# A four-layer retention kernel: both chunks' keys by values in one VectorE operation, a ring of four states, both states formed one behind the other

## What is computed

```python
Q = _rotate(Q, cos, sin); K = _rotate(K, cos, -sin)
att = jnp.einsum('bnhd,bmhd->bhnm', Q, K) * Dm      # Dm[n, m] = gamma**(n-m) for n >= m, else 0
Y = jnp.einsum('bhnm,bmhd->bnhd', att, V)
Y = (Y - mean) * rsqrt(var + EPS) ...
return G * Y @ Wo
```

## Time and profile before

| | us |
|---|---|
| median of 3 runs | 592.39 |
| the three runs | 592.39, 590.1, 597.42 |
| the profiled execution | 590.93 |
| its span, first to last instruction | 589.1 |
| mean granted TensorE clock, as a share of full speed | 0.979 |

### The profile page before, as it was taken

The page is one execution under the profiler, slowest core; times in us unless marked ns, Lnnn a source line. Parts: engine busy times, 40 slices in busy tenths (PEclk is TensorE's granted clock), DMA queues, the critical chain, the costliest instruction groups (busy, mean ns, idle before and its releaser), DMA issues. The chain is left out here.

```text
span 589.1 us, 13981 instructions
## 1 busy us (share of the span) xinstructions
PE 523.4 (89%) x4372; PEld 409.7 (70%) x4372; DVE 495.6 (84%) x1824; ACT 362.3 (61%) x830; POOL 214.1 (36%) x223
## 2 busy tenths in 40 slices
PE   0788999999999999999968896996499999897994
PEld 0656787878888888888856564994255777456992
DVE  6799999999999999999978897788958999993653
ACT  2577888787888887887747594686144310132760
POOL 2343543543543543543530073474200000072661
PEclk9899999999999999999999999899699999998998
DMA  8979999993000000000000311323000000012315
GB/s 305 364 201 187 182 171 183 181 177 59 3 1 2 2 3 2 2 2 2 2 1 2 116 47 54 87 65 104 0 0 1 2 0 2 0 52 59 101 56 160
DMA packets 61129, 43.29 MB, mean 73 GB/s; under 512 B 4640, under 2 KB 58272, under 8 KB 60800
## 3 DMA queue, kind: packets, MB, share of 16 engines
q1 hardware_dynamic: 56160, 35.42, 30.7%
q0 software_dynamic: 2496, 5.13, 2.6%
q10 hardware_dynamic: 2400, 1.84, 1.0%
HBM read 18.38 MB, written 24.01 MB: 72 GB/s over the span
## 5 line engine op out<-in xcount | busy, mean ns | idle before, releaser
L544 POOL TENSOR_TENSOR qk<-cosq,sinq 128x512 f32<-128x512 f32 x32 | 44.0, 1376 | 164.2 <-DVE cosq L865 164.2
L524 POOL TENSOR_TENSOR att<-att,small 128x512 f32<-128x512 f32 x63 | 79.0, 1275 | 10.2 <-ACT att L360 10.1
L368 ACT ACTIVATE xz<-resid,nmr,rs 128x128 f32<-128x128 f32 x128 | 53.1, 482 | 15.5 <-DVE nmr L921 15.4
L1234 POOL DMA_INDIRECT rows_back<-ffn_yt,ffn_front x46 | 47.8, 1038 | 40.5 <-DVE ffn_yt L1585 36.5
L1414 PE MATMUL banks<-ffn_xtT,ffn_wt 128*128 128x128 f32 x368 | 51.6, 286 | 2.0 <-DVE ffn_hr L1579 2.0
L1414 PEld LDWEIGHTS banks<-ffn_xtT,ffn_wt 128*128 128x128 f32 x368 | 47.1, 200 | 2.8 <-ACT ffn_wt L1261 2.2
L809 DVE TENSOR_TENSOR att<-banks,small 128x512 f32<-128x512 f32 x64 | 43.9, 685 | 4.9 <-PE banks L583 3.9
L1086 PE MATMUL banks<-small 128*128 128x512 f32 (+1 forms) x74 | 31.7, 547 | 13.6 <-POOL osc_taps L1657 11.5
L1225 POOL DMA_INDIRECT rows_in<-ffn_front,ffn_slot x32 | 31.9, 998 | 29.0 <-DVE ffn_slot L1497 20.5
L1217 POOL MEMSET ffn_all_one<- 128x8 f32 x2 | 0.2, 104 | 107.6 <-POOLq L1649 83.8
L360 ACT ACTIVATE att<-banks 128x512 f32<-128x512 f32 x63 | 37.9, 603 | 0.5 <-PE banks L583 0.5
(11 more groups left out here) (259 smaller groups left out, 1430.5 us busy)
## 6 DMA issues: line engine op xcount, KB each, us to landing
rows_in<-zero_rows SPq DMA_DIRECT2D x16, 1032.0 KB, 19.2
shared_tab<-in_rot SPq DMA_DIRECT2D x3, 1024.0 KB, 12.5
routed_sb<-in_routed SPq DMA_DIRECT2D x1, 3072.0 KB, 12.4
ffn_front<-rows_in SPq DMA_DIRECT2D x46, 64.5 KB, 1.8
ffn_yg<-rows_back SPq DMA_DIRECT2D x8, 256.0 KB, 3.7
shared_tab<-in_rot ACTq DMA_DIRECT2D x1, 1024.0 KB, 10.0
w<-in_W SPq DMA_DIRECT2D x2, 512.0 KB, 7.4
times<-in_times SPq DMA_DIRECT2D x1, 1024.0 KB, 4.9
```

Source lines behind the costliest of these rows:

```text
L368: ins = act.activation(xz[:, n], resid[:, (g % GROUPS) * 2 + n % 2], ACT.Identity, scale=rs[:, n:n + 1], bias=nmr[:, n:n + 1])
L524: pool.tensor_tensor(att[:, c, HALF:HEADS], att[:, c, HALF:HEADS], spread(causal.unsqueeze(1), 1, HALF), ALU.mult) \
L544: pool.tensor_tensor(qk[:, v].rearrange("p a b c -> p (a b c)"), cosq[:].rearrange("p a b -> p (a b)"), sinq[:].rearrange("p a b -> p (a b ...
L1234: pool.indirect_dma_start(rows_back, bass.IndirectOffsetOnAxis(ap=token, axis=0), yt[:, j % RING], None).then_inc(stored[j % RING], 16)
```

## The change

`keys_values` takes both chunks in one VectorE operation on 128 x 256 elements, with the mask repeated over the two chunks. Where a group is the last of its layer (first + 2 = 16, four groups of 32) the two chunks have different decays, and two operations stay, one behind the other. `kv_taken` counts groups and no longer chunks. The states go round in four buffers, and both `new_state` of a group stand one behind the other in the step in which its first stood before.

```diff
-        state = sb("state", [P, 2, D])
+        STATES = 4
+        state = sb("state", [P, STATES, D])
...
-                        pe.matmul(b_y[:, c * P:c * P + P], state[:, c], qkT[:, v, 0, c], start=(c == 0), stop=False,
+                        pe.matmul(b_y[:, c * P:c * P + P], state[:, (2 * g + c) % STATES], qkT[:, v, 0, c], start=(c == 0), stop=False,
...
-                            wait(pe, s["kv_taken"], 2 * (t - 1))
+                            wait(pe, s["kv_taken"], t - 1)
...
-                def keys_values(g, c):
-                    wait(dve, s["state_ready"], 2 * g + c - 1)
+                def keys_values(g):
+                    wait(dve, s["state_ready"], 2 * g)
                     wait(dve, s["kv_ready"], g + 1)
-                    dve.scalar_tensor_tensor(out=kvm[:, c], in0=b_og[:, c * P:c * P + P],
-                                             scalar=chunk_decay(g, c), in1=block,
-                                             op0=ALU.mult, op1=ALU.mult).then_inc(s["kv_taken"], 1)
+                    both = b_og[:, 0:2 * P].rearrange("p (c n) -> p c n", c=2)
+                    first = (2 * g) % NCH
+                    if first + 2 < NCH:
+                        dve.scalar_tensor_tensor(out=kvm[:], in0=both, scalar=decay[:, first:first + 1],
+                                                 in1=spread(block.unsqueeze(1), 1, 2),
+                                                 op0=ALU.mult, op1=ALU.mult).then_inc(s["kv_taken"], 1)
+                    else:
+                        for c in range(2):
+                            ins = dve.scalar_tensor_tensor(out=kvm[:, c], in0=both[:, c],
+                                                           scalar=decay[:, first + c:first + c + 1], in1=block,
+                                                           op0=ALU.mult, op1=ALU.mult)
+                        ins.then_inc(s["kv_taken"], 1)
 
                 def new_state(g, c):
-                    wait(dve, s["kv_taken"], 2 * g + c + 1)
+                    wait(dve, s["kv_taken"], g + 1)
                     wait(dve, s["state_ready"], 2 * g + c)
-                    wait(dve, s["state_read"], 2 * g + c)
-                    dve.scalar_tensor_tensor(out=state[:, 1 - c], in0=state[:, c],
-                                             scalar=chunk_decay(g, c), in1=kvm[:, c],
+                    wait(dve, s["state_read"], 2 * g + c - 2)
+                    n = 2 * g + c
+                    dve.scalar_tensor_tensor(out=state[:, (n + 1) % STATES], in0=state[:, n % STATES],
+                                             scalar=decay[:, n % NCH:n % NCH + 1], in1=kvm[:, c],
                                              op0=ALU.mult, op1=ALU.add).then_inc(s["state_ready"], 1)
...
-                        first_keys_values(t, u, on)
+                        keys_by_values_taken(t, u, on)
                         newton = chain_begun(t, on)
                         next(newton)
                         next(newton)
                         next(newton)
                         next(newton)
-                        second_state(t, u, on)
                         next(newton)
                         next(newton)
-                        second_keys_values(t, u, on)
                         last_masked(t, u, on)
-                        first_state(t, u, on)
+                        states(t, u, on)
                         next(newton)
                         chain_ended(t, newton)
                         means(t, u, on)
```

More of the change, by code:

```diff
@@ L685, in keys_by_values @@
                         else:
-                            wait(pe, s["kv_taken"], 2 * g)
+                            wait(pe, s["kv_taken"], g)
                         wait(pe, s["v_sb"], g + 1)
@@ L819, in masked_rest @@
                                       ALU.mult).then_inc(s["att_masked_rest"], 1)
-                def chunk_decay(g, c):
-                    return decay[:, bass.ds((g & (GROUPS - 1)) * 2 + c, 1)]
-                def keys_values(g, c):
-                    wait(dve, s["state_ready"], 2 * g + c - 1)
+                def keys_values(g):
+                    wait(dve, s["state_ready"], 2 * g)
                     wait(dve, s["kv_ready"], g + 1)
-                    dve.scalar_tensor_tensor(out=kvm[:, c], in0=b_og[:, c * P:c * P + P],
-                                             scalar=chunk_decay(g, c), in1=block,
-                                             op0=ALU.mult, op1=ALU.mult).then_inc(s["kv_taken"], 1)
+                    both = b_og[:, 0:2 * P].rearrange("p (c n) -> p c n", c=2)
[10 more added lines that the diff above has]
+                        ins.then_inc(s["kv_taken"], 1)
@@ L896, in aggregated, with keys_by_values_taken @@
                         ins.then_inc(s["bn_aggr_done"], 1)
-                def first_keys_values(t, u, on):
+                def keys_by_values_taken(t, u, on):
                     if on(2):
[L900 to L908, removed]
+                        keys_values(t - 2)
                 def last_masked(t, u, on):
@@ L912, in last_masked, with states @@
                         masked(t - 2, 0)
-                def first_state(t, u, on):
+                def states(t, u, on):
                     if on(2):
                         new_state(t - 2, 0)
+                        new_state(t - 2, 1)
                 def means(t, u, on):
```

## The result

The changed kernel takes 597.40 us (median of 20 runs, 591.1 to 601.56) where the kernel before takes 592.54 (20 runs beside them, 590.1 to 597.42). The ratio is 1.0078, 95% interval [1.0061, 1.0095]: slower, by less than the 2% that were named as the line between changed and unchanged. On two later occasions, on chips where the kernel before takes 620.6 and 620.8 us, the same pair gave 1.0020 [0.9995, 1.0044] and 1.0024 [0.9994, 1.0053]. The profiled execution took 595.9 us, its span is 594.1 (before 589.1), the mean granted clock 0.973 (before 0.979).

What follows compares the result with a forecast made beforehand. TensorE was taken to bound steady steps, VectorE early ones, a chain of waits step 33. Steady 0, early +0.32 and step 33 +0.38 gave +0.70 us on 591.66, so 592.4 us, range 588.9 to 597.0.

Steps and rivals of the forecast that it cites:

- What bounds the kernel: TensorE times steady steps 8 to 31, VectorE early steps 3 to 6, a chain of waits step 33.
- The place, +0.08: VectorE's stretch from `kvm` to `nmr`: 2.80 us before, forecast 2.88, bounds -0.16 and +0.35.
- the empty link: Chain link from L168 to L172, which a state had filled: forecast 0.21 us without it, 0.39 before.
- the second starts 0.38 after the first: In the changed place, the second state waits for the first: 0.38 us between starts, not 0.26.
- The bound of 0.47: Upper bound for the distance between the two states' starts: the longest such distance in the trace, 0.47 us.
- Steady steps, 0: Steps 8 to 31: 0.08 us later fits inside VectorE's 0.25 us of gaps ahead of L972, so no cost.
- The slow rival: Place grows past its cover, from 3.05 us steady steps lose time too: +4.3 us, 596.0 us; chance 0.12.
- Early steps, +0.32: Steps 3 to 6, paced by VectorE, each pay 0.08 us: +0.32 us, bounds -0.64 and +1.40.
- Step 33, +0.38: One state more between L809 and `nmr` at the end of the retention part: +0.38 us, bounds 0.26 and 0.47.
- The chain of waits in the earlier trace has no slack behind it: In step 33, time added ahead of `nmr` goes through the whole chain, so the extra state costs +0.38 us.
- Waits on the own engine are free: Rival: no cost for VectorE's waits on itself, early steps -0.13 us each, end +0.26: 591.4 us; chance 0.10.
- DVE sets the pace throughout: Rival: VectorE paces steady steps too, saving 0.16 us in each of 31 steps: -5.0 us, 586.7 us; chance 0.06.

Runs made afterwards that it cites:

- the kernel before with one more: Kernel before plus one VectorE operation of a state's shape in step 33, result never read: 593.52 us, 1.0020 [0.9990, 1.0050].
- the two takes: Changed kernel with two `kvm` operations in every group and four unread matmuls on TensorE in step 33: 623.39 us, 1.0043 [1.0019, 1.0068].
- one state less: Changed kernel without the second state of step 33, which nobody reads: 595.06 us beside 592.65, 1.0032 [1.0003, 1.0061].
- the first experiments: The first follow-up timings, 12 runs per kernel, beginning with one state less: 595.06 us beside the kernel before at 592.65.
- filled throughout: Unread matmuls on TensorE ahead of the first step, in steps 1 to 6 and 33: changed kernel 622.26 us (1.0020), kernel before 619.18 us (0.9975).
- before filled: Kernel before with four unread matmuls on TensorE in step 33: 619.60 us, 0.9993 [0.9966, 1.0020].
- filled: Changed kernel with four unread matmuls on TensorE in step 33: 593.35 us, 1.0006; timed again, 621.94 us, 1.0017.
- the states apart: Changed kernel with its first state moved ahead into the link behind L168, the second left behind: 591.39 us, 0.9999; later 619.49 us, 0.9977.

## Why the prediction was wrong

The forecast was 592.4 us with a range up to 597.0; the median is 597.4. Of the 5.0 between them 0.9 is the starting point, 591.66 where the kernel before has 592.54 over 20 runs; the change itself was forecast at +0.70 and came out at +4.9. Two steps failed: the price of a state that waits for the one just before it, and, by far the larger, TensorE's clock, which the prediction nowhere mentions and so put at nothing.

- *What bounds the kernel.* Right. Steady steps are timed by TensorE, early ones by VectorE, step 33 by the chain of waits; the steady period stayed at 8.83.
- *The place, +0.08.* It measured +0.20. Joined `kvm` to `vv` was forecast as 0.37 and is 0.37; the empty link as 0.21 and is 0.22. The mis-sized term is "the second starts 0.38 after the first": it is 0.46. I had carried 0.03 beyond the busy time over from links that are 22 wide and wait on one semaphore. With one semaphore, in the kernel before with one more, 0.38 was right; the changed kernel's second state has three waits, `kv_taken`, `state_ready` and `state_read`, and takes 0.46. Whether that is the reason, no run separates. The bound of 0.47 lies near it by luck: there the state doesn't read what the `kvm` ahead of it wrote, and the other 30 such distances of that profile are 0.26 or 0.27. The Trainium skill's rule ("VectorE: DVE Perf Modes", The DRAIN you can't avoid), by which a semaphore costs nothing extra, is further off: 0.26 by the rule, 0.46 in the trace. The page's row is of eight copies, and it doesn't say that each waits for the one before.
- *Steady steps, 0.* Right but for 0.13 us, which are lost in steps 8 and 9 (17.80 us together, 17.67 before), so that one step more than the four forecast ones paid; and with more room than I counted: 0.46 and not 0.25. The slow rival that "decides from a place of 3.05 us" fell at 3.10 with the two takes. Its time of 596.0 is near the result by accident; its mechanism isn't there.
- *Early steps, +0.32.* It measured +0.50 in the first pair of profiles and +0.70 over nine of them. The sign and the regime were right, the size is mostly the place's; that it comes near four times 0.20 is in part luck, since the place grew by 0.05 to 0.30 in these steps.
- *Step 33, +0.38.* The state brings `nmr` 0.44 later and makes TensorE's wait 0.44 longer, the same undersized term as above. That the period of step 33 grows by 0.39 is luck: against the changed kernel with one state less it grows by 0.69 (10.92 against 10.23), of which 0.47 are the state and the rest goes with the clock, and with one state less the step is 0.30 shorter than in the kernel before, since no `kvm` stands behind its `vv` any more. The step that failed is the sentence behind the term, "The chain of waits in the earlier trace rows has no slack behind it", which I took for the whole bill. In its place the runs showed that the clock fell behind the longer wait, in 4 profiles of 4, and step 34 then took 1.6 to 1.9 us more. It fell behind the old wait too, in 2 of 5, so the price is shown and its cause only in part.
- *The fast rivals.* "Waits on the own engine are free" fell with the 0.46; "DVE sets the pace throughout" fell with the steady period.

What this leaves of the sum: +0.7 early, +0.4 in step 33 and +1.8 beside the low clock in step 34 are +2.9 us, 0.5% of 592. The later two timings, +0.2% with intervals up to 0.44% and 0.53%, are near it; the first, +0.78%, is above it. What filled that up is not settled; the chips differ as well, 592 us there and 620 in the later two, and no run separates the chip from chance.

The mean clock of the timed runs points at more such falls: it was 0.9657 for the changed kernel and, beside the first experiments, 0.9751 for the kernel before (592.65 us), and within either kernel a run with 0.01 less is 3.3 to 3.8 us longer, so 0.0094 would stand for some 3 us. But timed runs leave no timeline, and where they lose the clock can't be seen. Against "the clock alone" stand the two kernels filled throughout: 622.26 changed and 619.18 before, 0.5% apart, with the clock at 1.00 behind step 33 in both profiles; but their mean clocks aren't equal either (0.9644 and 0.9684).

Of the two entries of the count outside the steps, the 1.11 ahead of step 2 is no effect of the order: the `vv` of step 2 starts anywhere between 20.7 and 22.9 us in the 17 profiles (before 20.93, before filled 22.15; changed 22.04 and 21.19, filled 20.97), and until the `kvm` just ahead of it only the longer memset is changed. The 0.9 behind the retention part is another matter: it goes with the second fall of the clock, which came with the extra operation in 4 profiles of 4. It cost 0.9 us in the changed kernel's profile and 5.1 in that of the kernel before with one more operation, and may well be where part of the missing time lies; timed runs can't show it.

No version beats the kernel before beyond its interval. The nearest are the states apart (0.9999 and 0.9977; 0.9981 [0.9959, 1.0003] filled throughout) and the kernel before filled throughout (0.9975 [0.9949, 1.0001]). Of the change, the joined operation shortens the place (2.70 instead of 2.80) if the states stay apart, though its own median shows no gain (1.0000 [0.9973, 1.0026]); with the states side by side the gain is less than they cost.

## What to carry to other kernels

When a step lengthens a wait of TensorE, look at the granted clock behind that wait, not only at how late the work comes: with 0.4 us more of waiting the next step took 1.8 us longer here. Give such a term a price and a chance even where the kernel before keeps its clock, and read the clock in several profiles, since one can't tell its fall from chance. Operations that depend on each other belong in the holes of another chain rather than side by side; here the same instructions took 3.00 us together and 2.70 apart. And where the trace has no row of the same kind for a wait, a difference carried over from a narrower operation with fewer semaphores is a guess: here 0.38 for 0.46.

## What the runs showed of the hardware that was not expected

- A 128x128 state that reads the one just before starts 0.44 to 0.46 us after it in the changed kernel, an operation that doesn't wait for the state 0.26; on 22 columns it is 0.21 against 0.10 to 0.12. In the kernel before with one more operation, which also reads the state just written but waits on one semaphore instead of three, it was 0.38 (297.92 to 298.30), and 0.27 to the next. So width alone doesn't give the 0.46, and the runs don't tell what does:

```profile
297.92 0.34 DVE L836 SCALAR_TENSOR_TENSOR state<-state,small,kvm 128x128 f32<-128x128 f32 x1
298.30 0.35 DVE L920 SCALAR_TENSOR_TENSOR spare<-state,small,kvm 128x128 f32<-128x128 f32 x1
298.57 0.17 DVE L178 SCALAR_TENSOR_TENSOR vt<-vt 128x22 f32<-128x22 f32 x1
```

- The granted clock falls or holds in one and the same program: the states apart had 1.00 and 0.50 in the stretch from 301 to 304 us in two profiles, of two chips. Within one chip the mean clock of the changed kernel's 20 runs goes from 0.956 to 0.975.
- A fall can come back later: 12 to 15 us behind the `vv` of step 38 the clock is 0.50 in all four unfilled profiles with the extra operation, and 1.00 in the five unfilled ones without.
- The whole kernel took 592.6 us on one chip and 620.4 to 620.8 on others. The retention part is the same on both: from step 2 to step 38 the changed kernel's two profiles have 306.24 and 306.35 us, in executions of 595.9 and 625.45 us. The difference lies behind it: from the `vv` of step 38 to the end of the span they have 265.8 and 295.0 us.
